# First layer: causal mask written into the scores' PSUM bank by ScalarE instead of by a TensorE product

## What is computed

```python
x = L0_attn_x
xn = _layernorm(x, axis=-1)
x = x + _L0_attn_ref(xn, ...) + _L0_ffn_ref(xn, ...)
xn = _layernorm(x, axis=-1)
x = x + _L1_attn_ref(xn, ...) + _L1_ffn_ref(xn, ...)
```

```python
scores = jnp.einsum('bqhd,bkd->bhqk', q, k) * scale
min_val = jnp.finfo(scores.dtype).min
causal = jnp.tril(jnp.ones((S, S), dtype=bool))
scores = jnp.where(causal[None, None], scores, min_val)
attn = jax.nn.softmax(scores, axis=-1)
ctx = jnp.einsum('bhqk,bkd->bqhd', attn, v)
```

## Time and profile before

| | us |
|---|---|
| runs, median of 3 (lowest to highest) | 1118.03 (1117.82 to 1121.88) |
| the profiled execution | 1118.86 |
| its span, first to last instruction | 1117.1 |
| first layer's 96 units, from the first mask product to the last of step 95, about | 28 to 362 |
| second layer and leftover of the first, about | 362 to 1117 |

### The profile page before, as it was taken

The page is one execution under the profiler, slowest core; times in us unless marked ns, Lnnn a source line. Parts: engine busy times, 40 slices in busy tenths (PEclk is TensorE's granted clock), DMA queues, the critical chain, the costliest instruction groups (busy, mean ns, idle before and its releaser), DMA issues.

```text
span 1117.1 us, 21334 instructions
## 1 busy us (share of the span) xinstructions
PE 1046.9 (94%) x7339; PEld 957.1 (86%) x7339; DVE 840.0 (75%) x1695; ACT 686.3 (61%) x1921; POOL 520.0 (47%) x626
## 2 busy tenths in 40 slices
PE   7678999899899789999999999999999999999996
PEld 6567779779778678888899999999999999999996
DVE  6677778887767658887777777777777777777774
ACT  3676776766665435555566666676666666555553
POOL 5596665654674000007843444534444433688100
PEclk9999999999999999999999999999999999999999
DMA  7746847756764286624544555455445542333120
GB/s 217 235 127 191 222 132 212 192 159 189 190 197 150 98 236 179 222 76 159 172 134 148 161 185 156 134 151 165 141 139 187 163 143 85 111 112 104 58 95 19
DMA packets 140282, 171.71 MB, mean 154 GB/s; under 512 B 11152, under 2 KB 103440, under 8 KB 139152
## 3 DMA queue, kind: packets, MB, share of 16 engines
q1 hardware_dynamic: 137104, 161.96, 48.0%
q0 software_dynamic: 3072, 8.39, 2.4%
HBM read 121.95 MB, written 48.37 MB: 152 GB/s over the span
## 4 chain that ended last, share of the span: by engine, by line
PE 66%; DVE 15%; ACT 7%; POOL 5%; issue 3%; DMA 3%; SPq 1%; DVEq 0%; ACTq 0%; POOLq 0%
PE ps_m L1684 26%; PE ps_s L1684 9%; PE ps_t L1684 7%; PE ps_b L1684 4%; ACT probs L498 3%; PE ps_b L845 3%; POOL d_xs L1320 3%; PE ps_t L1800 2%; PE ps_c L1684 2%; PE ps_c L1800 2%; DVE neg_max L787 2%; PE ps_t L910 2%; PE ps_m L845 1%; DVE pT L791 1%; DMA d_q_scr<-sT 1%
## 5 line engine op out<-in xcount | busy, mean ns | idle before, releaser
L1437 ACT ACTIVATE probs_a<-ps_s,neg_max_a 128x256 f32<-128x256 f32 x256 | 117.8, 472 | 143.2 <-DVE neg_max_a L1650 143.2
L1684 PE MATMUL ps_m<-xTa,w_qk 128*128 128x512 f32 x768 | 199.0, 398 | 4.2 <-DVE v L1503 1.6
L1684 PEld LDWEIGHTS ps_m<-xTa,w_qk 128*128 128x128 f32 x768 | 136.8, 188 | 34.5 <-issue 5.4
L498 ACT ACTIVATE probs<-ps_s,neg_max 128x128 f32<-128x128 f32 (+1 forms) x256 | 104.7, 420 | 57.1 <-DVE neg_max L787 55.8
L1650 DVE TENSOR_REDUCE neg_max_a<-ps_s 128x2 f32<-128x512 f32 x128 | 88.1, 691 | 46.8 <-PE ps_s L1684 45.2
L1337 POOL CAST we_down<-raw_down_e 128x256 fp32r<-128x256 f32 x47 | 18.7, 397 | 208.0 <-DMA raw_down_e<-in_we_down 208.0
L1684 PE MATMUL ps_m<-w_v,xTa 128*128 128x256 f32 x768 | 106.1, 287 | 0.0
L1684 PE MATMUL ps_t<-pTa,v 128*128 128x256 f32 x768 | 104.2, 285 | 0.0
L1684 PE MATMUL ps_s<-kTa,qTa 128*128 128x256 f32 x768 | 102.8, 283 | 0.3 <-DVE kTa L1473 0.2
L1684 PEld LDWEIGHTS ps_t<-pTa,v 128*128 128x128 f32 x768 | 97.7, 193 | 0.1
L1684 PEld LDWEIGHTS ps_s<-kTa,qTa 128*128 128x128 f32 x768 | 96.7, 192 | 1.0 <-DVE kTa L1473 0.7
(11 more groups left out here) (257 smaller groups left out, 2825.3 us busy)
## 6 DMA issues: line engine op xcount, KB each, us to landing
w_qk<-d_w_head SPq DMA_DIRECT2D x64, 512.0 KB, 4.0
raw_up<-in_we_up SPq DMA_DIRECT2D x47, 352.0 KB, 3.5
d_w_head<-parts SPq DMA_DIRECT2D x128, 128.0 KB, 2.8
raw_down_e<-in_we_down SPq DMA_DIRECT2D x47, 256.0 KB, 2.8
codes<-in_w_codes SPq DMA_DIRECT2D x64, 128.0 KB
scales<-in_w_scales SPq DMA_DIRECT2D x64, 128.0 KB
q<-d_q_scr SPq DMA_DIRECT2D x32, 256.0 KB, 5.5
d_xs<-zeros SPq DMA_DIRECT2D x16, 384.0 KB, 5.5
```

What stands on the lines that cost most here:

```text
L498: last = act.activation(probs[:, g % 3, a * w:(a + 1) * w], ps_s[g % 2][:, a * w:(a + 1) * w], ACT.Exp, bias=neg_max[:, g % 2, a:a + 1], s ...
L1437: last = act.activation(probs[:, s, t, :], ps_s[s][:, t * SEQ:(t + 1) * SEQ], ACT.Exp, bias=neg_max[:, s, t:t + 1], scale=1.0, accum_out=s ...
L1684: last = pe.matmul(out, lhs[i], rhs[j], start=start and n == 0, stop=stop and n == 2, skip_group_check=True)
```

## The change

GpSimd builds the mask into the right half of a tile `mask_wide`, 128 x 256, whose left half is zero. From unit 2 on, TensorE's mask product falls away. In its place ScalarE copies the mask, broadcast over the heads, over the whole bank (128 x 512, zeros for the first 128 keys of a `t == 1` unit) with a new function `seed`. It is the last work of ScalarE's step g and writes the bank of unit g+2. It waits for ScalarE's own exponentials of unit g to be complete. `scores(g)` then waits for the count `seeded` in place of `p_ok`, and its score products add to what is in the bank. Units 0 and 1 keep the mask product.

```diff
--- before.py
+++ after.py
@@ -94,7 +94,8 @@
     w_up = sb("w_up", [P, DC, HID], R32)
     xnT = [sb(f"xnT{i}", [P, DC, PAIR], R32) for i in range(2)]
     w_qkv = [sb(f"w_qkv{i}", [P, DC, D + P], R32) for i in range(2)]
-    nc.sbuf_base += 4 * 4 * PC
+    mask_wide = sb("mask_wide", [P, 2 * P])
+    nc.sbuf_base += 4 * (4 * PC - 2 * P)
     parts = [sb(f"parts{i}", [P, 2, PC], R32) for i in range(2)]
     gated = sb("gated", [P, 2, PAIR])
     xn = sb("xn", [P, TP, D])
@@ -147,7 +148,6 @@
     raw_qkv = sb("raw_qkv", [P, DC, QW])
     raw_gate = sb("raw_gate_l0", [P, DC, HID], I32)
     raw_up = sb("raw_up_l0", [P, DC, HID], I32)
-    mask_f = sb("mask_f", [P, P])
     assert nc.sbuf_base <= region_probs
     nc.sbuf_base = region_sums
     raw_down = sb("raw_down", [P, len(HT), D], I32)
@@ -270,6 +270,7 @@
     gate_up_ready, down_ready, late_high, late_ready = sem("gate_up_ready"), sem("down_ready"), sem("late_high"), sem("late_ready")
     var_ok = sem("var_ok")
     zero_ok = sem("zero_ok")
+    seeded = sem("seeded")
     cleared = sem("cleared")
     rstd_ok = sem("rstd_ok")
     ln_done = sem("ln_done")
@@ -415,12 +416,12 @@
     def gpsimd(pool):
         pool.memset(zeros[:], 0.0).then_inc(zero_ok, 1)
         pool.memset(ident[:], 0.0).then_inc(filled, 1)
-        pool.memset(mask_f[:], 0.0).then_inc(filled, 1)
+        pool.memset(mask_wide[:], 0.0).then_inc(filled, 1)
         pool.memset(minus_half[:], -0.5).then_inc(filled, 1)
         pool.wait_ge(filled, 3)
         pool.affine_select(out=ident[:], in_=ident[:], compare_op=ALU.not_equal, fill=1.0, base=0,
                            pattern=[[-1, P]], channel_multiplier=1).then_inc(const_ok, 1)
-        pool.affine_select(out=mask_f[:], in_=mask_f[:], compare_op=ALU.is_ge, fill=MASKED, base=0,
+        pool.affine_select(out=mask_wide[:, P:2 * P], in_=mask_wide[:, P:2 * P], compare_op=ALU.is_ge, fill=MASKED, base=0,
                            pattern=[[-1, P]], channel_multiplier=1).then_inc(const_ok, 1)
         for padded in (k3[:], v_wide[:]):
             pool.memset(padded.bitcast(F32), 0.0).then_inc(pads_zero, 1)
@@ -500,6 +501,14 @@
                                       accum_out=sums[:, 2 * s + t, h:h + 1])
             last.then_inc(p_ok.sem, 1)
 
+
+        def seed(g):
+            p, s, t, j, nj = units[g]
+            nh, w = DC * nj, (t + 1) * P
+            act.wait_ge(p_ok.sem, p_ok.at(0, g - 1))
+            act.activation(ps_s[g % 2][:].rearrange("p (h k) -> p h k", h=nh),
+                           mask_wide[:, 2 * P - w:2 * P].unsqueeze(1).to_broadcast([P, nh, w]), ACT.Copy).then_inc(seeded, 1)
+
         def high_probs(g):
             act.wait_ge(t_full.sem, t_full.at(0, g + 1))
             act.wait_ge(pv_ok.sem, pv_ok.at(0, g - 1))
@@ -563,7 +572,7 @@
             if item[0] == "q" and item[2] == 0:
                 act.wait_ge(const_ok, 2)
                 act.activation(ident_r[:], ident[:], ACT.Copy).then_inc(consts_r, 1)
-                act.activation(mask_r[:], mask_f[:], ACT.Copy).then_inc(consts_r, 1)
+                act.activation(mask_r[:], mask_wide[:, P:2 * P], ACT.Copy).then_inc(consts_r, 1)
                 act.wait_ge(small_ok, 3)
                 act.wait_ge(pads_zero, 2)
             early_item(item)
@@ -604,6 +613,8 @@
                     act.wait_ge(late_in, 16 * LATE_LOADS)
                     act.wait_ge(pads_zero, 3)
                 act.activation(high, raw, ACT.Copy).then_inc(late_high, 1)
+            if g + 2 < ALL:
+                seed(g + 2)
 
         for g in range(ALL):
             step(g)
@@ -891,12 +902,14 @@
             out = ps_s[g % 2]
             if g == 0:
                 pe.wait_ge(consts_r, 2)
+            if g >= 2:
+                pe.wait_ge(seeded, g - 1)
             if t == 0 and j == 0:
                 pe.wait_ge(item_done.sem, item_done.at(0, number["kv", p, s] + 1))
                 pe.wait_ge(q3_got[s], 64 * (p + 1))
-            pe.wait_ge(p_ok.sem, p_ok.at(0, g - 1))
             by_head = out[:].rearrange("p (h k) -> p h k", h=nh)
-            pe.matmul(by_head[:, :, t * P:w], ident_r[:], mask_r[:].unsqueeze(1).to_broadcast([P, nh, P]), start=True, stop=False, skip_group_check=True)
+            if g < 2:
+                pe.matmul(by_head[:, :, t * P:w], ident_r[:], mask_r[:].unsqueeze(1).to_broadcast([P, nh, P]), start=True, stop=False, skip_group_check=True)
             for a in range(nj):
                 last = pe.matmul(out[:, a * DC * w:(a + 1) * DC * w].rearrange("p (c k) -> p c k", c=DC),
                                  q3[:, s, j + a, t * P:(t + 1) * P], k3[:, s, :, 0:w],
```

## The result

Over 22 timed executions of each on one chip, the changed kernel took 1121.09 us (median; 1118.44 to 1124.85) and the kernel before 1118.57 us (1115.92 to 1121.88). The ratio is 1.0022 with an interval of 1.0015 to 1.003: **2.5 us slower**, within the 0.5% set as the bound, where 1.0 us was forecast. The profiled execution took 1120.50 us (span 1118.8) at a mean granted clock of 0.992, that of before 1118.86 (span 1117.1) at 0.996.

A forecast was written before the change was run, and what follows sets the result against it. A chain hopping between engines in the first layer, not TensorE's 89% busy time, was taken to set the end. Removal -3.3 and seeds +4.3 gave +1.0 us: 1119.9 against the profiled 1118.9, 1119.0 as a median; range 1115.5 to 1124.0.

The forecast's parts named there:

- the likeliest case: Whole kernel: an even exchange of removed mask products against added seeds, 1117.5 to 1121.5 us; chance 0.53.
- Removal, -3.3 us: First layer's chain: mask products on it total 3.75 us, less 0.47 for unit 0, which stays.
- the remaining 11.6 us: TensorE, first layer: the part of the mask products' 14.9 us off the chain, forecast to become idle time.
- Seeds, +4.3 us: ScalarE, first layer: delays where the chain passes its next instructions: start +1.0, copies +1.3 and +0.6, exponentials +1.4.
- the 1.0 at the start: Units 1 to 3: seeds of units 2 and 3 delay VectorE by 0.64 and some 0.36 us.
- the 27: Steps from 1 to 92 where ScalarE's two idle times sum to below 0.64 us; shortfalls total 8.1 us.
- its rule: ScalarE's queue: a seed vanishes if idle time before the next copy and before the next exponentials together exceeds 0.64 us.
- The weakest zero: TensorE: nothing added for transposes and items queued behind late scores, on which ScalarE and VectorE wait.
- Rival 3: First layer: ScalarE sets the pace, all 27 steps' shortfalls and late scores count, +7.9 us, 1126; chance 0.15.
- Rival 2: ScalarE's seed: a cheap write, so the removed products prevail, 1115.7 to 1117.5 us; chance 0.20.
- Rival 4: First layer: TensorE sets the pace, all 14.9 us of mask products come back, 1103 us; chance 0.02.
- Rival 5: Turns' joints: shifted weight transfers decide, 1 or 2 us either way, 1116 to 1121 us; chance 0.10.

## Why the prediction was right, and where its sum was off

**The result** lies in the range, on the side and within the bound of the likeliest case, at +2.5 instead of +1.0 us. That the sum came so close is in part luck: both terms were too large, and their errors have opposite signs. The gain was forecast at 3.3 us and measured at 0.0 alone, the cost at 4.3 and measured at 2.5; of the errors of 3.3 and 1.8 us, 1.5 is left.

**Removal, -3.3 us: the step that failed.** "The chain cannot get shorter than that by this removal alone" was not contradicted: the first layer ended 1.5 and 1.7 us earlier in two profiles without the mask products and 2.4 later in the third, whose clock fell twice. The step from there to the kernel, that its end moves by as much as the chain in the stage gets shorter, did not hold: 0.0, +0.8 and +3.3 us were measured. Also "the remaining 11.6 us become TensorE's idle time" was taken as harmless. The runs without mask products and seeds have a mean clock of 0.9779, 0.9780 and 0.9781, where before had 0.9799 to 0.9802 beside them. Among the executions of before, a clock lower by 0.001 goes with 0.43 to 0.67 us more; so by this estimate 0.002 stands for about 1 us, of the 1.5 that were given back in the first of them. That the falls are the cause is shown at single places (1.5 us each) and argued for the sum. It does not carry over to the kernels with seeds: the one with seeds in turns 2 to 4 has no lower clock (0.9805) and is not faster than before either. Where the gain goes in those is open. The scatter behind the first layer hides it: from the last maximum to the end it is 785 to 790 us in the four profiles from the first of these chips and 755 to 758 in the four from the second, in code that all have in common.

**Seeds, +4.3 us: too large.** Alone they measured +2.5 [1.0, 3.9]. The price of one seed was right; the step that a place on ScalarE's path passes its full delay on to VectorE's maxima was not:
- The price was 0.61 us, with 0.52 until the next instruction where something follows at once (126.12 to 126.64 below); 0.62 and 0.52 were forecast.
- The first turn was to hold nearly all the cost, and by the medians did (+2.1, against +0.6 for the other three turns together). But in the profile the maxima come only 0.24 us later behind the copy at 56 us and 0.51 behind that at 68, where 0.64 each was forecast, and of the 1.0 at the start 0.6 is there before a seed acts. The copies at 95 and 102 us move them by nothing and by 0.2 us, where 0.3 each was forecast.
- The exponentials at 111.81, 156.58 and 244.65 moved the maxima behind them by nothing, where 0.4 each was forecast, although seeds beside two of them stand on the chain after; behind those at 214.05 they come 0.1 us later, where 0.2 was forecast.
- Missed was 126 us (and 303), a delay of 0.34 us each. By instruction:

```profile
126.12 0.58 ACT L509 ACTIVATE ps_s<-mask_wide 128x512 f32<-128x512 f32 x1
126.64 0.58 ACT L515 ACTIVATE pT<-ps_t 128x512 fp32r<-128x512 f32 x1
...
127.25 0.69 DVE L802 TENSOR_TENSOR pT<-ps_t,pT 128x512 fp32r<-128x512 f32 x1 [0.25 <-ACT pT L515]
...
128.09 0.63 PE L923 MATMUL ps_t<-ident,probs 128*128 128x128 f32 x4 [0.44 <-DVE pT L802]
```

In before, the copy ended at 125.78 and VectorE took it up at 126.13: a slack of 0.35 us. ScalarE had no idle time before this copy and 0.47 us before the exponentials, so the step was among the 27; the forecast put it at nothing because the chain of before does not pass ScalarE there, and by its rule the shortfall was only 0.17 us. The rule counted idle time behind the copy; but a late copy is passed on by VectorE as soon as it exceeds VectorE's own slack. Everything from there on ran 0.34 us later, within a turn.

**ScalarE's busy time** grew by 47 us, not 58: where instructions overlap the time counts once, 94 x 0.5. Its waits came down to 58.7, close to the "some 50". TensorE's busy time fell by 8.5 us in the stage instead of 15. Only 0.5 of it fell in the first 74 us, where this profile's clock was 0.94 against 0.98; why the other turns gave 8.0 and not 11.5 was not looked into. Wrong, by the prediction's own list, would have been waits for `pT[1]` well over 21 us: they rose to 26.2.

**The weakest zero**, TensorE's late scores, was small: 2.3 us of waits of its products in 3 places, 1.8 of it at the start, in the sum already.

**Rival 3** did not come at one seed (+2.5, not +7.9) and did at two (+23.8): its mechanism is real, and this kernel stood closer to it than a busy share of 274 in 334 us suggests. **Rival 2**, a cheap write, is out by the 610 ns. The Trainium skill, "ScalarE: Activation LUTs", section "Step-by-step: what each stage is for", calls PSUM ScalarE's lower-latency destination; here the copy from SBUF takes 610 ns into PSUM and 0.64 us into SBUF, 0.03 us in its favour. **Rival 4**, all 14.9 us, is out by the removal alone. **Rival 5**, the transfers, was not tested by itself; the joints shift by up to 1.8 us either way in the profiles with at most one seed, and the intervals of all results are as wide.

No version tried beats the kernel before. The removal without anything in its place was measured at 0.0 us [-1.4, +1.5], so a cheaper way of writing the mask could be expected to bring 1.4 us at most.

## What to carry to other kernels

A few microseconds won in an early stage are not a few microseconds won at the end: measure the removal by itself, without its replacement, before the replacement is built. Moving work from a busy engine to one with idle time costs what the idle time cannot take at the places where the chain passes, and the slack to compare it with is that of the engine that takes up the result next, not of the engine that does the work. A piece's length on the new chain is not its cost either: 7.9 us of seeds stood on it and 2.5 were lost. That cost is far from linear (2.5 us for the first 0.6 us per unit, 21 for the second), and the place in the queue counts too (+2.5 or +6.3 us for the same seeds).

## What the runs showed of the hardware

- ScalarE's copy of 128 x 512 takes 601 ns from PSUM to SBUF and 610 ns from SBUF to PSUM: the direction hardly matters.
- The same TensorE wait of 2.17 us ahead of the same 18 products was followed by a fall of the clock to the lower level in 5 of 14 profiles, at a price of 1.5 us in the changed kernel's. A wait of 1.9 us was, in 4 of 8 places (1.0 to 1.5 us each), and one of 1.5 us in none of 18. Taking the mask products away without seeds in their place lengthened this wait from 1.51 to 1.90 us; in the change, with the seeds at the end of the step, it was 1.47.
